# A two-layer graph network on one core: span banks cleared by ScalarE, degree products in two parts, one chunk's maxima and the weights' row sums moved

## The reference

```python
# layer 0: attention over the edges of a node (three kinds of edges: 256, 1280, and 6656 in the last kind)
feat  = concat([h[src], h[dst]], axis=1)
e_f   = relu(feat @ W_kind + b_kind)                 # (8192, 2048) @ (2048, 1024)
logit = e_f @ W_a + b_a
m     = segment_max(logit, dst)
ex    = exp(logit - m[dst]);  den = segment_sum(ex, dst)
z     = segment_sum((ex / den[dst])[:, None] * h[src], dst)
x     = x + relu(concat([h, z], 1) @ W_n + b_n)      # W_hn for nodes 0-127, W_on for the others
# layer 1: h is the layernorm of the new x
w_out, w_in     = segment_sum(w, src), segment_sum(w, dst)
deg_out, deg_in = number of edges out of / into a node, at least 1
c     = w * rsqrt(w_out[src] * w_in[dst])
agg   = segment_sum(h[src] * rsqrt(deg_out)[src] * c, dst) * rsqrt(deg_in)
x     = x + relu(agg @ W + b)
```

## Time and profile before

| what | us |
|---|---|
| three runs | 643.57, 644.53, 636.51 |
| their median | 643.57 |
| the profiled execution, its own time | 641.69 |
| its span | 639.8 |
| TensorE busy | 575.2 (90%) |
| VectorE busy | 419.2 (66%) |
| ScalarE busy | 211.0 (33%) |
| GpSimd busy | 158.8 (25%) |

### The profile page before, as it was taken

How to read it: one execution, slowest core, us unless ns; L and a number is a source line. 1 busy time by engine, 2 the same in 40 slices (tenths; PEclk the granted TensorE clock), 3 DMA queues, 4 the chain that set the end, 5 groups by cost and what they waited for, 6 DMA issues and landing times.

```text
span 639.8 us, 7799 instructions
## 1 busy us (share of the span) xinstructions
PE 575.2 (90%) x2587; PEld 374.9 (59%) x2587; DVE 419.2 (66%) x692; ACT 211.0 (33%) x255; POOL 158.8 (25%) x153
## 2 busy tenths in 40 slices
PE   3989999999999978973399979699999999989997
PEld 2868888444444333421144456476668888868885
DVE  6966457378695997593978586636663276686235
ACT  4511444996716151001001661101424062315110
POOL 3200000577745555442565200000000000021000
PEclk9989999999999989998599988779997998999999
DMA  8974831899999999999599941031000735304002
GB/s 332 389 274 161 280 113 59 293 411 410 410 414 411 360 404 415 410 410 407 179 407 409 410 155 34 1 98 71 1 2 2 262 119 178 98 1 131 1 33 99
DMA packets 43655, 144.83 MB, mean 226 GB/s; under 512 B 5409, under 2 KB 5729, under 8 KB 43617
## 3 DMA queue, kind: packets, MB, share of 16 engines
q1 hardware_dynamic: 22000, 69.22, 29.3%
q0 software_dynamic: 18432, 67.12, 26.6%
q10 hardware_dynamic: 3184, 7.99, 3.3%
HBM read 131.70 MB, written 12.62 MB: 226 GB/s over the span
## 4 chain that ended last, share of the span: by engine, by line
PE 50%; DVE 21%; DMA 12%; POOL 5%; issue 5%; ACT 4%; DVEq 2%; ACTq 1%; POOLq 0%
PE banks L1064 19%; DMA rows<-table,ids_i 9%; PE banks L1156 7%; PE banks L1127 7%; PE banks L1218 7%; POOL rows L429 5%; DVE masked L776 4%; DVE rows L754 4%; PE banks L1235 3%; DVE rows L755 3%; PE banks L1170 3%; ACT pick_src L541 1%; ACT pick_src L545 1%; DMA lift<-lift_row 1%; DVE stats L653 1%
## 5 line engine op out<-in xcount | busy, mean ns | idle before, releaser
L429 POOL DMA_INDIRECT rows<-table,ids_i x124 | 139.2, 1123 | 184.6 <-DMA table<-stage 84.0
L1084 PE MATMUL banks<-w_raw,fT_raw 128*128 128x512 f32 x384 | 168.5, 599 | 11.5 <-issue 4.7
L1084 PEld LDWEIGHTS banks<-w_raw,fT_raw 128*128 128x128 f32 x384 | 73.0, 191 | 106.4 <-issue 94.2
L754 DVE TENSOR_TENSOR rows<-rows 128x1024 f32<-128x1024 f32 x62 | 75.7, 1221 | 54.3 <-DMA rows<-table,ids_i 49.4
L663 DVE TENSOR_TENSOR w_lo<-w_raw,w_hi 128x1024 fp32r<-128x1024 f32 x40 | 48.4, 1223 | 58.5 <-ACT w_hi L472 57.7
L1064 PE MATMUL banks<-w_hi,fT_hi 128*128 128x512 f32 x200 | 80.2, 401 | 3.0 <-DVE w_lo L663 3.0
L1064 PE MATMUL banks<-w_lo,fT_hi 128*128 128x512 f32 x200 | 79.9, 399 | 0.0
L1064 PE MATMUL banks<-w_hi,fT_lo 128*128 128x512 f32 x200 | 79.5, 397 | 0.0
L755 DVE SCALAR_TENSOR_TENSOR rows<-rows,wa_rep 128x1024 f32<-128x1024 f32 x62 | 75.9, 1225 | 2.1
L1127 PE MATMUL banks<-w_raw,fT_raw 128*128 128x512 f32 x128 | 58.2, 617 | 20.0 <-DVE xf L808 20.0
L472 ACT ACTIVATE w_hi<-w_raw 128x1024 fp32r<-128x1024 f32 x40 | 41.7, 1058 | 89.8 <-PE banks L1064 78.8
(11 more groups left out here) (168 smaller groups left out, 665.4 us busy)
## 6 DMA issues: line engine op xcount, KB each, us to landing
w_raw<-in_L_gnn_W_ho_dram SPq DMA_DIRECT2D x16, 512.0 KB
table<-stage SPq DMA_DIRECT2D x32, 256.0 KB, 6.9
w_raw<-in_L_gnn_W_oo_dram SPq DMA_DIRECT2D x16, 512.0 KB
w_raw<-in_L_gnn_W_on_dram SPq DMA_DIRECT2D x16, 512.0 KB
w_raw<-in_L_gnn_W_hn_dram SPq DMA_DIRECT2D x16, 512.0 KB
w_raw<-in_L_gnn_W_hh_dram SPq DMA_DIRECT2D x16, 512.0 KB
w_raw<-in_L_gnn_W_dram SPq DMA_DIRECT2D x8, 512.0 KB
lift<-lift_row ACTq DMA_DIRECT2D x7, 512.0 KB
```

What stands on the lines that cost most here:

```text
L429: pool.indirect_dma_start(out=rows[:, slot, side, :], out_offset=None, in_=table[kind][side], in_offset=bass.IndirectOffsetOnAxis(ap=ids_i ...
L754: step(dve.tensor_tensor(rows[:, r, 0, :], rows[:, r, 0, :], rows[:, r, 1, :], ALU.add))
L1084: ins = pe.matmul(bank[j][:, :], fT_raw[:, k, m * P:(m + 1) * P], w_raw[:, c % SLOTS, n * H:(n + 1) * H], start=(k == 0), stop=(k == K - 1))
```

## The change

Six edits. (1) The opening product of zeros of every span goes; ScalarE writes zeros into the bank instead (`clear_bank`), for spans 0 and 1 after `keep_edges(1)` and for span n+2 behind `keep_span(n)`, once that copy is complete; `add_span(n)` waits for `bank_clear`. (2) The degree products of tiles 16 to 63 start once 24 pairs are made; those of tiles 0 to 15 come behind `add_span(3)`. (3) `chunk_max(6)` moves from behind `lift_chunk(7)` into the loop, at c = 62: behind edge 59 and ahead of edges 60 and 61. (4) The last chunk's maxima, the node maxima, the exponentials and their parts come four or so spans earlier. (5) The row sums of the weights go from behind the last fold to between `products(C_BOT + K, ...)` and the second `features`, into bank 0; VectorE waits for them and copies them ahead of `second_h(0)`. (6) `in_sums` goes behind `second_h_lo(B - 1)`.

```diff
-        MAX_AFTER = (27, 32, 37, 42, 47, 57)
-        LAST_MAX, ME_PE, ME_DVE, PARTS, EXP = 4, 7, 9, 11, 7
+        MAX_AFTER = (27, 32, 37, 42, 47, 57, 62)
+        LAST_MAX, ME_PE, ME_DVE, PARTS, EXP = 3, 3, 5, 7, 3
...
                 act.activation(span_sum[n % 2][0:3 * SPAN, :], bank[4 + n % 2][0:3 * SPAN, :], ACT.Copy).then_inc(span_out, 1)
+                if n + 2 < 2 * SPANS:
+                    act.wait_ge(span_out, n + 1)
+                    clear_bank(n + 2)
+
+            def clear_bank(n):
+
+                act.activation(bank[4 + n % 2][0:3 * SPAN, :].rearrange("p (a c) -> p a c", c=P),
+                               zeros[0:3 * SPAN, None, :].broadcast_to([3 * SPAN, N // P, P]), ACT.Copy).then_inc(bank_clear, 1)
...
                     keep_edges(1)
+                    act.wait_ge(hh_raw_done, K)
+                    for n in range(2):
+                        clear_bank(n)
...
             lift_chunk(NC - 1)
-            chunk_max(NC - 2)
...
                 low_of(adjT_lo, s, bank[s][:, :], adjT_hi, adjT_hi_done, s + 1, adjT_lo_done)
-                if s == 0:
-                    dve.wait_ge(wsum_done, 1)
-                    dve.tensor_copy(wsum[:, :], bank[7][:, 0:B]).then_inc(wsum_kept, 1)
...
             out_sums()
-            in_sums()
...
                 low_of(adjT_lo, s, adjwT[:, s, :], adjT_hi, adjT_hi_done, B + s + 1, adjT_lo_done)
+            dve.wait_ge(wsum_done, 1)
+            dve.tensor_copy(wsum[:, :], bank[0][:, 0:B]).then_inc(wsum_kept, 1)
             second_h(0)
...
             second_h_lo(B - 1)
+            in_sums()
...
-            def degrees():
+            def degrees(tiles, opens=False, closes=False):
...
-                for q in range(T):
+                for q in tiles:
...
-                if n >= 2:
-                    pe.wait_ge(span_out, n - 1)
-                pe.matmul(out_bank[rows3, :], zeros[:, rows3], node_no, start=True, stop=True)
+                pe.wait_ge(bank_clear, n + 1)
                 pe.wait_ge(span_ready, n + 1)
...
             pe.wait_ge(hh_raw_done, K)
+            pe.wait_ge(src_made, EARLY_SRC)
+            degrees(range(T // 4, T), opens=True)
             pe.wait_ge(src_made, T // 2)
-            degrees()
             for n in range(2 * SPANS):
                 add_span(n)
                 if n:
                     fold_span(n - 1)
                 if n == ME_PE:
+                    degrees(range(T // 4), closes=True)
+                if n == ME_PE:
                     node_maxima()
             fold_span(2 * SPANS - 1)
-            for m in range(B):
-                for s in range(B):
-                    ins = pe.matmul(bank[7][:, m:m + 1], adjwT[:, s, m * P:(m + 1) * P], ones_f[:, 0:1],
-                                    start=(s == 0), stop=(s == B - 1))
-            ins.then_inc(wsum_done, 1)
...
-                        if i == 0 and first_layer and f == K - 1:
+                        if i == 0 and not first_layer and f == 0:
                             pe.wait_ge(wsum_kept, 1)
...
             products(C_BOT + K, range(BLOCK_H, B), keep=True)
+            pe.wait_ge(x2_step, 1)
+            for m in range(B):
+                for s in range(B):
+                    ins = pe.matmul(bank[0][:, m:m + 1], adjwT[:, s, m * P:(m + 1) * P], ones_f[:, 0:1],
+                                    start=(s == 0), stop=(s == B - 1))
+            ins.then_inc(wsum_done, 1)
             pe.wait_ge(adjT_lo_done, 2 * B)
             features(range(B), B, B, False)
```

More of the change, by code:

```diff
@@ L228, in build @@
         lift_ready = sem("lift_ready"); lift_out = sem("lift_out"); last_out = sem("last_out"); lift_in = sem("lift_in"); max_done = sem("max_done")
-        span_ready = sem("span_ready"); span_full = sem("span_full"); span_out = sem("span_out"); folded = sem("folded"); deg_done = sem("deg_done"); src_made = sem("src_made"); own_act = sem("act_step");
+        span_ready = sem("span_ready"); span_full = sem("span_full"); span_out = sem("span_out"); bank_clear = sem("bank_clear"); folded = sem("folded"); deg_done = sem("deg_done"); src_made = sem("src_made"); own_act = sem("act_step");
         sums_out = sem("sums_out"); wsum_done = sem("wsum_done"); wsum_kept = sem("wsum_kept"); den_done = sem("den_done"); den_kept = sem("den_kept"); rden_ready = sem("rden_ready"); fdst_ready = sem("fdst_ready"); adjwT_ready = sem("adjwT_ready")
@@ L1131, in _ @@
                 ins.then_inc(chunk_used, 1)
-            def degrees():
+            def degrees(tiles, opens=False, closes=False):
                 regions = bank[6][:, 0:4 * B]
-                pe.matmul(regions, zeros[:, :], node_no[:, 0:4 * B], start=True, stop=True)
-                for q in range(T):
+                if opens:
+                    pe.matmul(regions, zeros[:, :], node_no[:, 0:4 * B], start=True, stop=True)
+                for q in tiles:
                     for s in range(B):
@@ L1140, in degrees @@
                                   start=False, stop=True, skip_group_check=True)
-                pe.matmul(regions, zeros[:, :], node_no[:, 0:4 * B], start=False, stop=True,
-                          skip_group_check=True).then_inc(deg_done, 1)
+                if closes:
+                    pe.matmul(regions, zeros[:, :], node_no[:, 0:4 * B], start=False, stop=True,
+                              skip_group_check=True).then_inc(deg_done, 1)
             def add_span(n):
```

## The result

The changed kernel is slightly slower: 644.53 us (median of 20 runs) against 641.02 for the kernel before (20 runs), a ratio of 1.0055 with a 95% interval of 1.0029 to 1.0082, or 3.5 us. That lies inside the stated range, 632 to 649, but I had forecast 1 us gained, and the loss is clear of noise: by its sign the prediction was wrong.

What follows compares the result with a forecast made beforehand. It took TensorE or VectorE, whichever comes last in each stage, as the bound. Gains of 11.7 and 5.5 less 15.9 lost made 1.3 us, 641.69 to 640.4, stated as 640.5; range 632 to 649.

Steps and rivals of the forecast that it cites:

- Stage 3, row sums ahead of the second features: After the weight products, VectorE waits for the moved row sums, delaying `second_h(0)` and the eighth bank: 15.9 us lost.
- Rival B: At the second features, VectorE's wait for the row sums costs little: 626 us, chance 0.06.
- Stage 2: Behind the last fold, layer 0's features start earlier without the row sums: 5.5 us gained (4.2 to 6.9).
- Stage 1, maxima of chunk 6: Before span 1, maxima start at 365.3 in VectorE's gather waits; span 1 starts 4.1 us earlier.
- Rival A: Chunk 6's lift lands late, each microsecond past 365.3 lost; 4 us late gives 644.4 us; chance 0.14.
- Stage 1, early degrees: Before span 0, 192 degree products take 5.3 us from 374.1; alone they bring nothing beyond span 1's start at 386.3.
- Stage 1, last maxima: After span 3, node maxima run from 399.0 to 405.6; the 5.42 us wait shrinks to 0.8.
- Stage 1, openers: In spans 4 to 25, dropping the opening product saves 0.16 us each: period 2.95 against 3.11.
- if the spans keep a period of 3.1, the openers: Check on the changed profile: a span period still at 3.1 us would show the opener saving to be wrong.
- the other end: In the spans, dropping openers saves nothing, with VectorE's loop 0.16 us longer than thought.
- Rival C: In the spans, ScalarE's clears delay its copies and the folds by 0.3 us a span: 648 us, chance 0.08.
- opener term: Saving over the spans from dropping the opening products, 0.16 us a span, counted as 3.5 us.

Runs made afterwards that it cites:

- experiment 2: Changed kernel with ScalarE copying the row sums and VectorE's wait and copy ahead of `second_h(0)` gone: 633.83 us, ratio 0.9873 to the kernel before.
- Experiment 1: Changed kernel with the weights' row sums, VectorE's copy of them and `in_sums` back where they stood before: 631.38 us, ratio 0.9896 to the kernel before.
- experiment 4: Changed kernel with constants in place of TensorE's loop and both registers in the spans: 636.69 us, ratio 0.9964 to the kernel before.
- experiment 6: Kernel before, openers kept, with constants in place of TensorE's loop and registers in the spans: 634.41 us, ratio 0.9906.
- experiment 5: Changed kernel with one of two register-held addresses per span product replaced by constants, loop kept: 639.39 us, ratio 1.0016 to the kernel before.
- 7: Changed kernel with both ScalarE's copy of the row sums and constants in TensorE's spans: 625.11 us, ratio 0.9781 to the kernel before.

## Why the prediction was wrong, point by point

- **Stage 3, row sums ahead of the second features: right.** Forecast: a wait of VectorE of about 15 us, the eighth bank 19.0 us behind it, TensorE idle about 7 us, row sums 3.6 us at full clock. Measured: 15.21, 19.03, 6.99 and 3.8. Taken out alone (experiment 2) the wait gave 12 us back by the timed runs and 15 by the profile. Rival B, that the wait would cost little, is out.
- **Stage 2: right.** The features started 1.50 us behind the last fold's adjacency, as forecast; the granted clock stood at half from about 481 to 484.4, so that eight products or so took 0.43 us instead of 0.23, 1.6 us in all against the 1.3 that I had taken. Stages 2 and 3 together: 10.5 us lost, forecast 10.4. Experiment 1 gives 10.
- **Stage 1, maxima of chunk 6: right.** They began at 363.75, 2 us behind edge 59, and their data had been fetched at 355.7, so it landed in 8.0 us as the earlier one. Rival A (late landing) did not happen.
- **Stage 1, early degrees:** the sum gave them no gain of their own beyond span 1, and the single profile nearly agrees (1.4 us); the timed runs give them about 5 us. Not settled.
- **Stage 1, last maxima: right in place, a little too hopeful.** Span 4 began at 405.4, forecast 405.6, but counted from `spread(0)` that is 31.9 us against 30.3. One reading was off without effect: chunk 7's fetch was issued 5.1 us behind its lift only because it had to wait for chunk 6's maxima there; with these gone it came 2.5 us behind.
- **Stage 1, openers: wrong, and this is the step that turned the sign.** I had "0.16 saved a span, not 0.24", 22 spans at 2.95 us from 405.6 to 474.4. Measured: 3.21 us a period; from span 4 at 405.4 the last fold ended at 479.2, 73.8 us where the sum had 68.8. The prediction had named this sign itself: "if the spans keep a period of 3.1, the openers". I looked for what would be late once the opener was gone and found VectorE's loop (3.75 us from the end of one span to the start of the next but one), but not the sequencer of TensorE itself, though its marks stood in the rows of before: the same eight products took 1.89 us in one span and 2.16 in the next, and a load of weights waited for "issue". With constants in place of the registers they took the same time in every span at full clock, 1.92 (experiment 4) and 1.89 (experiment 6, from span 9 on, but for one of 1.94). What I gave as the other end, "nothing saved at all", was the value to take, though I had put it down to VectorE's loop. Experiment 4 then shows that 0.4 us a span are there, in the loop and its registers.
- **Rival C, ScalarE's clears in the way:** not seen in the changed kernel. The clears took 0.60 us, behind the copy by 0.03, and no copy was late for a fold by more than 0.2 us. Where the sequencer is partly relieved they do come last now and then: three waits of 0.40 to 0.56 us in experiment 5. The 0.02 to 0.1 us a period by which spans without openers are slower than those with them (3.21 and 3.17 against 3.11 and 3.15) is too small to give it a cause here.

With the opener term at zero instead of 3.5 us the sum comes to 2.2 us lost, and with 3.21 us for all 22 spans to 4.4; measured were 3.5.

## What to carry to other kernels

Before an instruction is taken off an engine, ask whether the array or the instruction stream in front of it is late: equal products with unequal times, or idle time put down to "issue" inside a burst, pointed to the stream here, and then fewer columns bought nothing while fewer registers did. And when work is moved into another engine's gap, its reader moves too: choose as reader an engine that is idle there, because a wait for four columns holds back everything queued behind it.

## What I had not expected of the hardware

- A register-addressed loop of eight products costs TensorE's instruction stream more than eight products of 512 columns and a fold cost its array: 3.1 to 3.2 us a span with registers, 2.95 with half of them, 2.67 to 2.81 with constants. Taking the opener out of the array then did not shorten the period (3.21 against 3.11 with it). That it is the sequencer rests on these three kernels and the instruction counts of their pages; no trace shows the sequencer's own time.
- The number of early spans that run at half clock changes between kernels whose programs are the same up to the last fold: three in experiment 4 and five in 7, at 3.65 us for products that take 1.92 otherwise. Each is worth 1.7 us, as much as the effects that were looked for, so one profile of a kernel is no measure of a few microseconds.
